# First chunk's output projection and cross attention moved into the last head group of self attention

## What is computed

```
x = layernorm(x + causal_self_attention(x) @ Wout.T + bout)
q, k, v = x @ Wq + bq, ctx @ Wk + bk, ctx @ Wv + bv          # 16 heads
x = layernorm(x + softmax(q k^T / sqrt(32) + mask * -1e9) v @ Wo + bo)
logits = cosine(x, centroids) + x @ w_route.T;  gates = softmax over the top 2 of 8
x = layernorm(x + sum_e gates_e * (gelu(x @ w1_e + b1_e) @ w2_e + b2_e))
```

## Time and profile before

| | |
|---|---|
| median of 3 runs | 2510.7 us (2510.66 to 2512.7) |
| profiled execution | 2513.39 us |
| its span | 2511.5 us |
| PE busy in the span | 2360.9 us (94%) |
| DVE, ACT, POOL busy | 1600.6, 1180.6, 1133.6 us |

### The profile page before, as it was taken

The page is one execution under the profiler, slowest core; times in us unless marked ns, Lnnn a source line. Parts: engine busy times, 40 slices in busy tenths (PEclk is TensorE's granted clock), DMA queues, the critical chain, the costliest instruction groups (busy, mean ns, idle before and its releaser), DMA issues. The chain is left out here.

```text
span 2511.5 us, 36490 instructions
## 1 busy us (share of the span) xinstructions
PE 2360.9 (94%) x13524; PEld 998.4 (40%) x13524; DVE 1600.6 (64%) x3854; ACT 1180.6 (47%) x2197; POOL 1133.6 (45%) x454
## 2 busy tenths in 40 slices
PE   7999799999999999999955899999999999999998
PEld 3444222323333333333212445445445454445443
DVE  4443497777777777777506375757567675657664
ACT  4332156666676666666641344333435243433431
POOL 0000269999999999999971212111211212111100
PEclk9999799999999999999978899999999999999999
DMA  7874402121212122131003101010010101010000
GB/s 244 296 236 159 126 6 73 31 73 36 73 36 68 48 56 58 46 99 39 23 18 152 47 1 48 17 48 17 1 64 1 64 1 48 17 48 17 1 18 17
DMA packets 130478, 155.05 MB, mean 62 GB/s; under 512 B 19854, under 2 KB 98190, under 8 KB 129277
## 3 DMA queue, kind: packets, MB, share of 16 engines
q1 hardware_dynamic: 130301, 152.72, 19.7%
HBM read 99.99 MB, written 52.17 MB: 61 GB/s over the span
## 5 line engine op out<-in xcount | busy, mean ns | idle before, releaser
L762 ACT ACTIVATE probs<-st_ps 128x512 f32<-128x512 f32 (+3 forms) x1280 | 609.1, 535 | 330.3 <-PE st_ps L865 179.2
L637 POOL TENSOR_TENSOR total<-total,probs 128x2048 f32<-128x2048 f32 (+3 forms) x200 | 706.3, 3532 | 47.1 <-ACT probs L762 26.4
L804 DVE TENSOR_REDUCE seg_max<-s_ps 128x1 f32<-128x512 f32 x768 | 505.9, 685 | 134.5 <-PE s_ps L851 132.3
L865 PE MATMUL st_ps<-q_pair,k_pair 98*128 98x512 f16 (+3 forms) x1280 | 434.0, 352 | 26.8 <-ACT probs L762 15.2
L851 PE MATMUL s_ps<-k_pair,q_pair 96*128 96x512 f16 (+3 forms) x1280 | 434.9, 355 | 25.8 <-DMA q_pair<-q_parts 10.7
L1475 PE MATMUL fps<-x2T,w_p_hi 128*128 128x512 f16 x1024 | 318.6, 379 | 0.0
L1475 PE MATMUL fps<-w_p_hi,hT 128*128 128x512 f16 x1024 | 304.7, 379 | 2.8 <-DVE x L1429 1.7
L885 PE MATMUL o_ps<-probs,v_sb 128*32 128x512 f32 (+3 forms) x2560 | 301.6, 544 | 0.0
L808 DVE CUSTOM_DVE_ANT_0 s_ps<-s_ps,later 128x384 f32<-128x384 f32 (+3 forms) x512 | 249.1, 499 | 68.0 <-issue 67.8
L1158 POOL TENSOR_TENSOR soft<-soft,ssum 128x1232 f32<-128x1232 f32 x32 | 71.6, 2247 | 417.3 <-DVE ssum L1320 417.3
L865 PEld LDWEIGHTS st_ps<-q_pair,k_pair 98*128 98x128 f16 x1280 | 123.2, 97 | 326.8 <-ACT probs L762 226.5
(11 more groups left out here) (172 smaller groups left out, 3320.0 us busy)
## 6 DMA issues: line engine op xcount, KB each, us to landing
k_pair<-k_parts SPq DMA_DIRECT2D x96, 128.0 KB, 4.5
q_pair<-q_parts SPq DMA_DIRECT2D x96, 128.0 KB, 5.1
x_raw<-xT_in SPq DMA_DIRECT2D x8, 1024.0 KB, 6.0
q_parts<-qk_out SPq DMA_DIRECT2D x32, 256.0 KB, 3.5
k_parts<-qk_out SPq DMA_DIRECT2D x32, 256.0 KB, 3.6
piece_raw<-w_in SPq DMA_DIRECT2D x8, 1024.0 KB, 8.6
v_rows<-v_out SPq DMA_DIRECT2D x32, 256.0 KB, 2.1
w_parts<-piece_cut SPq DMA_DIRECT2D x8, 1024.0 KB, 5.5
```

The lines of the kernel that those rows point to most:

```text
L637: last = nc.gpsimd.tensor_tensor(summed[:, :, off:], other[:, :, off:], probs[:, k % NP, :, off:], ALU.add)
L762: nc.scalar.activation(probs[:, k % NP, h, off:], st_ps[:, p % (2 * NVU) % RING, off:], ACT.Exp, scale=SCALE).then_inc(exp_done.sem, 1)
L804: nc.vector.reduce_max(highest, s_ps[:, slot], AX.X).then_inc(s_read.sem, 1)
L865: last = nc.tensor.matmul(st_ps[:, slot, off:], k_pair[a][:, h, kt * P:(kt + 1) * P], q_pair[a][:, c, h, off:], start=True, stop=not diagonal)
```

## The change

The first chunk's stages out to pv3 no longer stand in the second block. They stand in the last lap of attention, at fixed steps given by a table, counted from the first unit of the last chunk (unit 64 is behind its last). The remaining stages (from out2) stay at the start of the second block. For that

- the chain's code becomes functions per engine (`pe_work` and so on) that both blocks use, and its semaphores are made before attention;
- in attention its banks are the three of s_ps, free after the last maximum (`banks_free`), in place of four of cps;
- tiles that both need (soft, work, kv) are made first; attention's q_pair0, k_pair0 and v_sb0, and project's x_raw and piece_raw lie in them;
- in the last chunk of the last group PE sums all 16 tiles into den_ps, POOL adds none, there are no totals; the first three tiles are summed 12, 10 and 8 units later, not 6;
- the context is loaded 40 units before the last chunk, and the first `bias_rows` stands 100 units before it;
- b2 is loaded at the start of the second block, ahead of the expert weights.

The core of the diff:

```diff
+    OPENING_SUMS = 12, 10, 8
+    def at_end(i, k):
+        return i == LAPS - 1 and k >= 2 * NKU - (CPB * TT)
+    def pooled(i, k):
+        return k % NKU in POOLED[KU[k % NKU][0]] and not at_end(i, k)
+    def first_at(who, s, end):
+        return [piece for at, *piece in first_chain[who] if end is not None and s == 2 * NVU - CPB * TT * HG + at]
...
-        q_pair = [sb(f"q_pair{a}", [NM, CPB, HG, CH], F16) for a in range(2)]
-        k_pair = [sb(f"k_pair{a}", [NM, HG, T], F16) for a in range(2)]
-        v_sb = [sb(f"v_sb{a}", [P, T // P, P], F32) for a in range(2)]
+        q_pair = [S["soft"][0:NM].rearrange("p j h s -> p (j h s)")[:, 0:CPB * HG * CH // 2].bitcast(F16).rearrange(
+            "p (c h n) -> p c h n", c=CPB, h=HG), sb("q_pair1", [NM, CPB, HG, CH], F16)]
+        k_pair = [S["work"][0:NM].rearrange("p a n -> p (a n)").bitcast(F16).rearrange("p (h t) -> p h t", h=HG),
+                  sb("k_pair1", [NM, HG, T], F16)]
+        v_sb = [S["kv"][:].rearrange("p (t f) -> p t f", f=P), sb("v_sb1", [P, T // P, P], F32)]
...
+        first_chain["banks"] = s_ps
+        first_chain["banks_free"] = s_read.sem, s_read.at(LAPS - 1, 2 * NAUX - 1)
...
             def step(i, s, first, end):
                 k = tile_at(s, 1, first, end)
-                if k is not None and k % NKU in ADDS:
-                    c, n = KU[k % NKU][0], adds_upto(k) - 1
+                if k is not None and k % NKU in ADDS and pooled(i, k):
+                    c, n = KU[k % NKU][0], adds_upto(i, k) - 1
...
+                for piece in first_at("pool", s, end):
+                    chain(-1, 1, *piece)
...
+                for piece in first_at("sp", s, end):
+                    sp.wait_ge(pv_done.sem, pv_done.at(i, NKU - 1))
+                    chain(*piece)
...
             def sums(i, k):
                 c, kt = KU[k % NKU]
-                if k % NKU in POOLED[c]:
+                if pooled(i, k):
                     return
-                opens = all(n in POOLED[c] for n, (x, _) in enumerate(KU) if x == c and n < k % NKU)
+                whole = at_end(i, k)
+                opens = kt == 0 if whole else all(n in POOLED[c] for n, (x, _) in enumerate(KU) if x == c and n < k % NKU)
+                off = max(kt - c * TT, 0) * P
                 if opens:
                     pe.wait_ge(den_taken.sem, den_taken.at(i, k // NKU * CPB + c - 1))
                 for h, out in enumerate(heads):
-                    last = nc.tensor.matmul(den_ps[out, :], ones[:], probs[:, k % NP, h], start=opens, stop=False)
+                    last = nc.tensor.matmul(den_ps[out, off:], ones[:], probs[:, k % NP, h, off:], start=opens,
+                                            stop=whole and k % NKU == LAST_TILE[c])
                 last.then_inc(pv_done.sem, 1)
...
+    SECOND = STAGES.index("out2")
+    VALUE = ("probs0", "probs1", "pv0", "probs2", "pv1", "probs3", "pv2", "pv3")
+    value_at = [(87 + n, stage) for n, stage in enumerate(VALUE)]
+    first_chain = {
+        "sp": [(-40, 0)],
+        "pool": [(-100, "rows"), (12, "out"), (60, "scores1"), (66, "scores2"), (72, "scores3")] + value_at,
+        "act": [(24 + j, "turn1", j) for j in range(TT)] + [(37 + 3 * o, "query", o) for o in range(KT)]
+        + [(57, "scores0"), (63, "scores1"), (67, "scores2"), (71, "scores3")] + value_at,
+        "dve": [(-2, "out"), (14, "norm1"), (24, "turn1"), (50, "scores0"), (56, "scores1"), (62, "scores2"),
+                (66, "scores3")] + value_at,
+        "pe": [(4 * j - 2, "out", j) for j in range(TT)] + [(22 + j, "turn1", j) for j in range(TT)]
+        + [(34 + 3 * o, "query", o) for o in range(KT)]
+        + [(50, "scores0"), (56, "scores1"), (62, "scores2"), (66, "scores3")] + value_at,
+    }
...
         def run(engine, slot, weights_used=False):
-            slot(-1, 1, with_experts=False)
+            slot(-1, 1, with_experts=False, start=SECOND)
...
-            start_stored(sp, stored)
-            load_context(0)
-            for dst, src in weights:
-                sp.dma_start(dst, src).then_inc(w_loaded, 16)
-            load_next(-1, 1)
+            def rest():
+                start_stored(sp, stored)
+                for r in range(3):
+                    sp.dma_start(b2_sb[r * GP:r * GP + E], b2).then_inc(b2_loaded, 16)
+                for dst, src in weights:
+                    sp.dma_start(dst, src).then_inc(w_loaded, 16)
+                load_next(-1, 1)
...
             def chain_bank(i, u, k):
-                if k >= CB:
-                    who = USES[k - CB]
-                    c, n = (act_read if who == "act" else dve_read), nth(USES, k - CB)
+                if in_first(i, u, k) and k < FCB:
+                    pe.wait_ge(*first_chain["banks_free"])
+                    return chain_out(i, u, k)
+                back = FCB if in_first(i, u, k) else CB
+                if k >= back:
+                    who = USES[k - back]
+                    c, n = (act_read if who == "act" else dve_read), nth(USES, k - back)
```

More of the change, by code:

```diff
@@ L777, in step @@
                     nc.scalar.activation(o_out[:, c % 2, 0], o_sb[:], ACT.Copy).then_inc(o_hi_done.sem, 1)
+                for piece in first_at("act", s, end):
+                    chain(-1, 1, *piece)
+            chain, begin, _ = first_chain["work"]["act"](act)
+            begin()
             for n in range(AHEAD):
@@ L822, in step @@
                     nc.vector.reciprocal(inv_small[:, c % 2], inv_small[:, c % 2]).then_inc(recips.sem, 1)
-            dve.wait_ge(made, 7)
+                for piece in first_at("dve", s, end):
+                    chain(-1, 1, *piece)
+            chain, begin, _ = first_chain["work"]["dve"](dve)
+            begin()
+            dve.wait_ge(made, 5)
             for n in range(AHEAD):
@@ L929, in step @@
                     aux(i, n)
+                for piece in first_at("pe", s, end):
+                    chain(-1, 1, *piece)
+            chain, begin, _ = first_chain["work"]["pe"](pe)
+            begin()
             pe.wait_ge(const_ready, 2)
@@ L1060, in chain_slot, with chain_out, in_first @@
             return ((2 * i + u) * NUSE + k) % CB
+        def chain_out(i, u, k):
+            if in_first(i, u, k):
+                return first_chain["banks"][:, k % FCB]
+            return cps[:, chain_slot(i, u, k)]
+        def in_first(i, u, k):
+            return 2 * i + u < 0 and k < AT_O
         def experts_slot(i, u, f):
@@ L1150, in chain @@
             def chain(i, u, stage):
-                if stage == "out":
+                if stage == "rows":
+                    bias_rows(chunk(i, u))
+                elif stage == "out":
                     pool.wait_ge(varied.sem, at(varied, i, u, 0))
@@ L1194, in chain @@
                     k0, dst = (AT_T1, x1T) if stage == "turn1" else (AT_T2, x2T[p])
[L1195 removed]
+                    for j in parts:
                         bank = wait_product(i, u, k0 + j)
@@ L1199, in chain @@
                 elif stage == "query":
-                    for o in range(KT):
+                    for o in parts:
                         bank = wait_product(i, u, AT_Q + o)
@@ L1476, in product, with chain @@
                 return last
-            def chain(i, u, stage):
+            def chain(i, u, stage, only=None):
+                parts = range(TT) if only is None else [only]
                 p = parity(u)
@@ L1486, in chain @@
                         k0, w = AT_O, W["wo_p"]
-                    for j in range(TT):
+                    for j in parts:
                         bank = chain_bank(i, u, k0 + j)
@@ L1559, in experts, with rest @@
                 last.then_inc(f_ready.sem, 1)
-            run(pe, program(chain, experts), weights_used=True)
+            def rest():
+                run(pe, program(chain, experts), weights_used=True)
+            return chain, begin, rest
+        first_chain["work"] = {"sp": sp_work, "pool": pool_work, "act": act_work, "dve": dve_work, "pe": pe_work}
+        attention(first_chain)
+        for name, shape in (("w1_p", [P, KT, E * DE]), ("w2_p", [P, FT, D])):
+            W[name] = [sb(f"{name}_{s}", shape, F16) for s in ("hi", "lo")]
@@ new lines, in chains @@
+        x2, x2T = ([sb(f"{name}_{a}", shape, dt) for a in range(2)]
+                   for name, shape, dt in (("x2", [P, TT, D], F32), ("x2T", [P, 2, KT, CH], F16)))
+        hidden, hT = sb("hidden", [P, 2, CH], F32), sb("hT", [P, 2, 2, 2, CH], F16)
+        stats3, agg3, rstd3 = sb("stats3", [P, TT, 6], F32), sb("agg3", [P, TT, 2], F32), sb("rstd3", [P, TT], F32)
+        square, rnorm = sb("square", [P, TT], F32), sb("rnorm", [P, TT], F32)
+        logit, weight = sb("logit", [P, TT, E], F32), sb("weight", [P, TT, E], F32)
@@ new lines, in chains, with _ @@
+        fps = stack.enter_context(nc.psum_tensor("fps", [P, FB, CH], F32))
+        cols = lambda t: t.rearrange("p t n -> p (t n)")
```

(7 more changed lines are left out.)

229 lines of the change are left out of this document (119 added, 110 removed).

## The result

The changed kernel takes 2484.66 us, median of four runs (2480.36 to 2485.55), against 2510.68 (2510.46 to 2512.7) for the kernel before on the same chip: ratio 0.9883, 95% interval 0.9872 to 0.9895. The prediction was 2483.2. The profiled execution has a span of 2483.2 us, 28.3 less than the earlier trace rows.

A forecast was written before the change was run, and what follows sets the result against it. PE is nearly full except at the seam, idle beside POOL's adds and the first chunk's lone chain. The terms move X from 1425.4 to 1397.9, so 2510.7 - 27.5 = 2483.2 us; range 2468 to 2497.

The forecast's parts named there:

- X: Start of the next chunk's first out product on PE, full from there: forecast to move from 1425.4 to 1397.9.
- The bias adds ahead of the last group: Four bias adds on POOL delay the totals, so PE stands 3.5 us; bounds 0 and 5.
- The last chunk: Fifth unit at 1253.2, then 56.1 us to scores0 at 1309.3, with 2.3 for the fourth transpose's wait on three banks.
- Rival B: In-order queues hold scores back at PE's chain waits, 1 us for each of ten or so pieces: 2493; chance 20%.
- rival D: New waits halve the granted clock: 5 us slower if over 33 us of work, 2562 if all; chance 3%.
- rival C: PE waits on softmax until the chain runs in effect behind the last chunk: -0.3, 2510.4; chance 3%.
- Softmax: First chunk's softmax on DVE and POOL: 27.7 us plus 3.5 of waits, probabilities done at about 1341.5.
- The port: DVE and POOL lock each other out during the softmax: up to 2.5 us later, left out of the sum.
- Values and the seam: Value products after the probabilities, 1.2 for bank waits, attention ends 1359.1; then 6.8 to PE's next block.
- S: Start of the second block on PE: forecast at 1365.9.
- Second block: From S to X: the next chunk's loads queue behind the expert weights, so X comes 32 us after S.
- Rival A: The next chunk's loads share the DMA engines and land unqueued: 6.5 us less, 2476.7; chance 15%.

The follow-up runs named there:

- e8: The changed kernel run again without an edit: 2484.9 us, ratio 0.9885.
- e3: The changed kernel with the first chunk's four bias adds on POOL one at a time at later steps, instead of all four together: 2480.4 us, ratio 0.9869.
- e7: The changed kernel with two of the maxima's banks for the first chunk's products instead of three: 2492.0 us, ratio 0.9919.
- e2: The changed kernel with the last chunk's adds back on POOL, PE without the sums, the chain kept inside: 2487.9 us, ratio 0.9900.
- e4: The changed kernel with the next chunk's loads issued after ten of sixteen expert weights, PE's weight wait moved to the first expert unit: 2478.1 us, ratio 0.9862.
- e5: The changed kernel with the first chunk's query and scores stages at earlier steps of the last chunk: 2477.3 us, ratio 0.9856.

## Why the prediction was right, step by step

The time came out 1.5 us over the forecast (2484.7 against 2483.2), X 1.3 under it (1396.59 against 1397.9). The parts that move X were named rightly: the chain under the chunk, the tail gone, the late bias adds, the loads behind the weights. That it came within 1.5 us is partly luck, since several terms were wrong and cancel: the last chunk began 3.3 us late and took 3.2 less, softmax, values and seam took 2.0 less, the second block 0.5 more. The two differences have opposite signs because the profiled execution of the kernel before (2513.39) was 2.7 us above its median and that of the changed one (2485.55) 0.9 above: X moved by 28.8, the median by 26.0.

**The bias adds ahead of the last group: the mechanism right, the size short.** Forecast: totals 3.5 us late, at about 1187. The timeline of POOL in the changed kernel:

```profile
1182.02 4.95 POOL L1201 TENSOR_TENSOR keep_x<-keep_x,keep_bout_bc 128x512 f32<-128x512 f32 x4
1186.94 1.25 POOL L654 TENSOR_TENSOR total<-total,probs 128x512 f32<-128x512 f32 x1
```

and of PE behind it:

```profile
1188.25 1.30 PE L948 MATMUL den_ps<-total,ones 128*32 128x512 f32 x8 [3.12 <-POOL total L654]
```

The four adds went in front of the last add of the group before, as said, and PE stood 3.12 us. But the next output is written 46.85 us behind the mark instead of 42.10: 4.75 later. The windows of the changed kernel behind the stand, with the granted clock third from the end of each row, say where the rest is:

```profile
1188.00:1190.00 2.00, 1.75 (x11) 0.50 (x12) 0.00 (x0) 0.09 (x1) 2.00 (x2) 0.74 0.00 0
1190.00:1192.00 2.00, 2.00 (x16) 0.89 (x14) 1.29 (x2) 1.25 (x5) 2.00 (x2) 0.50 0.01 1
1192.00:1194.00 2.00, 2.00 (x12) 0.71 (x8) 1.12 (x5) 1.25 (x3) 1.85 (x2) 0.91 0.07 12
```

The clock was still full while PE stood (1.00 in 1186 to 1188). It went to its lower level (1.2 of 2.4 GHz) 0.7 us after PE had gone on and stayed there for 3.4 us of full work. What that work lost by it is 2 x (0.26 + 0.50 + 0.09) = 1.7 us, and 3.12 + 1.7 = 4.8. In e8 the clock fell during the same stand (3.13, until 1189.67; 0.72 in 1188 to 1190), and a longer stretch at half clock followed:

```profile
1190.00:1192.00 2.00, 2.00 (x11) 0.34 (x4) 0.00 (x0) 0.03 (x1) 2.00 (x1) 0.50 0.00 0
1192.00:1194.00 2.00, 2.00 (x16) 0.89 (x14) 1.23 (x2) 1.31 (x5) 1.86 (x3) 0.50 0.00 0
1194.00:1196.00 2.00, 2.00 (x11) 0.68 (x6) 0.70 (x3) 0.73 (x2) 2.00 (x1) 0.57 0.06 12
```

By the same sum these cost 1.00 + 1.00 + 0.86, with 0.16 from before them 3.0, and 3.13 + 3.0 = 6.1; the lag was 5.85. The prediction priced the idle time and forgot the clock that an idle time costs; its upper bound of 5 was too low for e8. e3 took the term away: PE was 4.4 us earlier behind it, X 4.6.

**The last chunk: a wait that didn't stay.** The prediction kept PE's wait at the start of the chunk and hid two out pieces in it at no cost. PE's scores of units 5 to 7 before, and of units 4 to 6 in the changed kernel:

```profile
1249.73 1.58 PE L865 MATMUL st_ps<-q_pair,k_pair 98*128 98x512 f16 x3 [2.98 <-ACT probs L762]
```

```profile
1256.28 0.82 PE L901 MATMUL st_ps<-q_pair,k_pair 98*128 98x512 f16 x3
```

The wait is not there any more, nor the half clock that followed it before (0.50 in 1252 to 1254): the two out pieces, 2.6 us each, stand in its place and are longer than it. Unit 5 ran at about 1256.5 where 1253.2 was forecast: 1.2 of the 3.3 us by the mark, 1.2 by the stand, 0.8 by the out pieces. From there to scores0 56.1 us were forecast and 52.9 measured (to 1309.44). The 2.3 us for the fourth transpose with three banks was the wrong size: 0.34, in the row shown under e7. 0.8 more is a unit too many in the sum: from unit 5 to unit 50 are 45 units, 11.25 tiles, not 11.5. DVE had the first scores at 1310.29; 1310 was forecast, since the late start ate what these gave. Rival B (each chain piece 1 us) fell with PE's 81.86 of 83, rival D (the clock) with its 1.00, rival C with both.

**Softmax.** DVE of the changed kernel:

```profile
1310.29 1.96 DVE L1378 SCALAR_TENSOR_TENSOR keep_soft<-s_ps,keep_kv 128x308 f32<-128x308 f32 x4 [26.70 <-PE s_ps L1592]
...
1316.98 2.03 DVE L1378 SCALAR_TENSOR_TENSOR keep_soft<-s_ps,keep_kv 128x308 f32<-128x308 f32 x4 [1.78 <-PE s_ps L1592]
...
1323.51 1.77 DVE L1378 SCALAR_TENSOR_TENSOR keep_soft<-s_ps,keep_kv 128x308 f32<-128x308 f32 x4
...
1329.78 1.77 DVE L1378 SCALAR_TENSOR_TENSOR keep_soft<-s_ps,keep_kv 128x308 f32<-128x308 f32 x4
```

One wait of 1.78 where 2.5 + 1.0 were forecast; from the third stage DVE is full and PE waits for it, 2.62 us at 1330.25, as said. The last probabilities came 30.4 us after DVE's start (1340.66), 31.5 were forecast. The port was rightly left out of the sum, but not for the reason given there: all four subtractions took 1.44 because no POOL operation stood beside them. The scaling of chunk 2 (1278.81) and its low part (1309.67) came before the first subtraction. In e2, with the adds on POOL, three of the four took longer.

**Values and the seam.** From 1340.66 to the last bias add's end at 1357.65 are 17.0 us (17.6 forecast), the two bank waits 0.82 for 1.2. The last chunk's scaling stood behind it (1357.61), and PE began the next block at 1364.09, 6.5 later (6.8 forecast). S came 1.8 us before its forecast.

**Second block.** X - S was forecast at 32.0 and is 32.5. That term, the largest that no row of before showed, held: SP issued x at 1378.27, when out2 had been read, POOL stood 10.70 us for it, PE 6.75 in front of X. Rival A (the loads land unqueued) fell: 15.1 and 17.8 us to landing against 5.6 and 8.2. e4 shows that it is the place in the queue that sets it. By the Trainium skill (DMA: Bandwidth & Descriptors, "Queues, rings and completion order") the transfers that one engine issues are consumed in order on its ring of each DMA engine; the landing times of the changed kernel and of e4 agree. The prediction reads 5.7 us for the load of x where the earlier trace rows has 5.6, which changes nothing.

**What was not settled.** The profiles of one kernel differ by 1 to 2 us at X - mark (220.4 and 222.2 for the changed one), 1.1 of it the half-clock stretch behind the stand; where the steps of a microsecond ahead of the mark come from wasn't tried.

## What to carry to other kernels

When work moves into a full stretch, look at what it pushes in the queues that it shares: here four adds of 1.2 us on POOL cost 4.75, and sixteen weight loads in front of one that is needed cost 8, each got back by moving a few lines of order. Don't add up the parts of a change by what each brings alone: the sums alone brought 9.7 us and the chain alone 24.0, together 30.0, not 33.7, as both take the same tail off the path. When work is added on an engine, look at what it excludes on its neighbour: here adds on POOL cost the chain on DVE 4 to 6 us. Price a stand of PE at its idle time plus the half-clock stretch behind it (here 3.1 us and 1.7 to 2.7).

## What the runs showed of the hardware

Two things I had not expected. A stand of 3.1 us on PE took the granted clock to 0.5 in all six profiles that had it. In two of them (the changed kernel and e4) the clock fell 0.7 and 1.3 us after PE had gone on and was back after 3.4 us of half-clock work: 4.7 us in all. In four (e2, e5, e7, e8) it fell while PE stood and was back after 5.7 to 6.1 us of it: 5.8 to 5.9. Why it falls earlier or later isn't shown. And issuing a load on SP is not always short: behind the sixteen weights the issue itself took microseconds; in the changed kernel:

```profile
1378.27 0.38 SPq L988 DMA_DIRECT2D keep_x<-x_rows_in  x1
1378.69 3.59 SPq L989 DMA_DIRECT2D keep_oT<-o_parts  x1
1382.32 7.23 SPq L1161 DMA_DIRECT2D keep_kv<-k_blocks  x1
```

Before, the same three took 0.38, 0.51 and 0.58 us, and behind ten weights, in e4, 0.38, 0.51 and 2.10. Two small loads of the next chunk stood behind them, issued at 1389.60 and 1390.03, and nobody was waiting for those.
